# Fourteen gathered and eighteen dense columns per tile in the first layer of a two-layer graph network

## The reference, cut to what matters

```python
def layer0(x, W, b, src, dst):
    neigh_sum = segment_sum(x[src], dst, num_segments=N)
    deg = segment_sum(ones(E), dst, num_segments=N)
    mean = neigh_sum / maximum(deg, 1)[:, None]
    agg = where(deg[:, None] > 0, mean, x)
    return relu(concatenate([x, agg], -1) @ W.T + b)

x1 = layernorm(x + layer0(x, W, b, src, dst))
# layer 1: Q, K, V = x1 times a matrix chosen by node type; K of an edge also times a matrix
# chosen by edge type; softmax of Q[dst].K over the edges of each dst; sum of V[src] by it
out = layernorm(x1 + layer1(x1, src, dst, edge_type, node_type, ...))
```

## Time and profile before

| | |
|---|---|
| time, median of 3 runs | 3719.31 us (3719.02 to 3729.1) |
| time of the profiled execution | 3697.22 us |
| span of the profiled execution | 3695.4 us |
| mean granted TensorE clock | 0.839 of full speed |
| busy share | PE 69%, POOL 64%, DVE 41%, ACT 30% |
| first layer's steps, start to end | 99.4 to 1334.7 us |

### The profile page before, as it was taken

The page is one execution under the profiler, slowest core; times in us unless marked ns, Lnnn a source line. Parts: engine busy times, 40 slices in busy tenths (PEclk is TensorE's granted clock), DMA queues, the critical chain, the costliest instruction groups (busy, mean ns, idle before and its releaser), DMA issues.

```text
span 3695.4 us, 38864 instructions
## 1 busy us (share of the span) xinstructions
PE 2551.0 (69%) x13692; PEld 1754.7 (47%) x13692; DVE 1530.9 (41%) x4283; ACT 1124.1 (30%) x2072; POOL 2372.2 (64%) x2400
## 2 busy tenths in 40 slices
PE   1688888888888861666666666666676666666667
PEld 0355555555555541444444444444444444444445
DVE  8466666666666620222222222222222222222223
ACT  3333444444444420222222222222222222222222
POOL 6656667676666617566666666666666666666662
PEclk9799999999999985777777777777777777777778
DMA  4233344443444313233333333333333333333331
GB/s 135 64 98 115 107 130 120 119 120 107 120 120 120 112 68 107 72 96 96 97 97 96 97 97 96 97 97 96 97 97 97 97 97 96 96 97 97 97 97 43
DMA packets 195810, 369.81 MB, mean 100 GB/s; under 512 B 62177, under 2 KB 126509, under 8 KB 189347
## 3 DMA queue, kind: packets, MB, share of 16 engines
q0 software_dynamic: 112432, 281.92, 27.5%
q1 hardware_dynamic: 76679, 82.09, 6.7%
q10 hardware_dynamic: 6508, 3.33, 0.3%
HBM read 299.89 MB, written 67.30 MB: 99 GB/s over the span
## 4 chain that ended last, share of the span: by engine, by line
PE 38%; another core or an unknown queue 20%; issue 19%; ACT 14%; DVE 8%; ACTq 1%; DMA 0%; DVEq 0%; POOLq 0%; POOL 0%; SPq 0%
PE banks L715 8%; ACT work L1090 5%; PE banks L872 4%; PE banks L886 4%; PE banks L901 3%; PE banks L708 3%; ACT work L1098 3%; ACT picks L1007 2%; PE banks L738 2%; DVE sums L1269 2%; PE banks L771 1%; PE banks L908 1%; PE banks L866 1%; PE banks L776 1%
## 5 line engine op out<-in xcount | busy, mean ns | idle before, releaser
L655 POOL DMA_INDIRECT ring<-kv_table,src_n x1264 | 1207.9, 956 | 625.9 <-issue 368.8
L650 POOL DMA_INDIRECT ring<-x_part_rows,work x512 | 538.0, 1051 | 249.2 <-issue 138.4
L886 PE MATMUL banks<-identf,ring 128*128 128x128 f32 x1264 | 242.9, 319 | 646.5 <-ACT work L1098 458.2
L1007 ACT ACTIVATE picks<-banks 128x392 bf16<-128x392 f32 x800 | 396.6, 499 | 730.0 <-PE banks L708 646.7
L715 PE MATMUL banks<-sums,picks 128*128 128x385 bf16 x2450 | 617.6, 335 | 0.4 <-ACT picks L1007 0.4
L886 PEld LDWEIGHTS banks<-identf,ring 128*128 128x128 f32 x1264 | 169.4, 162 | 698.9 <-ACT work L1098 506.4
L1090 ACT ACTIVATE work<-banks,negmax 128x2048 f32<-128x2048 f32 x98 | 193.0, 1969 | 905.9 <-issue 668.4
L1098 ACT ACTIVATE work<-banks 128x512 f32<-128x512 f32 x392 | 213.0, 598 | 816.1 <-remote 689.1
L1467 DVE SCALAR_TENSOR_TENSOR sums<-sums,corr,banks 128x128 f32<-128x128 f32 x98 | 34.0, 347 | 936.5 <-remote 928.9
L1448 DVE TENSOR_REDUCE largest<-banks 128x1 f32<-128x2048 f32 x98 | 224.6, 2292 | 468.9 <-PE banks L872 252.3
L872 PE MATMUL banks<-work,queries 128*128 128x512 f32 x784 | 412.2, 674 | 4.1 <-issue 4.1
(11 more groups left out here) (279 smaller groups left out, 2785.7 us busy)
## 6 DMA issues: line engine op xcount, KB each, us to landing
kv_table<-ring SPq DMA_DIRECT2D x49, 1024.0 KB
ring<-kv_table,src_n POOLq DMA_INDIRECT x1264
ring<-x_part_rows,work POOLq DMA_INDIRECT x512
sums<-kv_table,src_n POOLq DMA_INDIRECT x304
x_part_rows<-sums SPq DMA_DIRECT2D x7, 675.5 KB, 4.5
src_n<-x_part_rows,work POOLq DMA_INDIRECT x256
sums<-x_rows SPq DMA_DIRECT2D x51, 64.0 KB, 1.9
x_rows<-ring SPq DMA_DIRECT2D x49, 64.0 KB
```

What stands on the lines that cost most here:

```text
L650: pool.indirect_dma_start(near[k % RUNS][:, j, :], None, part_dram, bass.IndirectOffsetOnAxis(ap=col_ids[:, first + j:first + j + 1], axis ...
L655: pool.indirect_dma_start(kv_ring[u][:, j, :], None, table, bass.IndirectOffsetOnAxis(ap=of, axis=0)).then_inc(l1_rows[2 * u + j // RUN], 16)
L886: tr = pe.transpose(bank[KEY_BANK[g]][:, j * P:(j + 1) * P], kv_ring[k.u][:, g * 4 + j, 0:D], identf[:, :])
L1007: act.activation(picked[:, par, :, c * NW:(c + 1) * NW], bank[c % 2][:, 0:KEYS].rearrange("p (h w) -> p h w", w=NW), ACT.Copy).then_inc(pi ...
```

## The change

- `NW` 8 to 7: a dense column covers 7 nodes. `GCOLS` 16 to 18: a dense group has 18 columns, 18 x 7 = 126 slots, so that `slot_sum` multiplies 126 of the 128 columns of weights, and a pick has 49 x 7 = 343 columns.
- Each tile has a fixed period of 32 columns: 14 gathered (two runs of `HALF` = 7), then 18 dense. All 49 steps are alike; the 50th is gone, and step 0 has runs too. The first layer gathers 686 columns in place of 768 and picks 882 in place of 800.
- `hot` works in batches of 3 with a ring of 9. The picks are spread evenly over the 49 slot sums (`PICK_AT` = 0, 3, 6, 9, 11, 14, ... 41, 44, 47). The runs stand at h=2 and 23, `node_sum` at 6, the parts of `late` at 9 to 29, those of `early` at 30, 36 and 42.
- DVE's order: after `join_parts` come `hot(i+1, 2)`, `belong`, `add_nodes`, `mean`, then the other batches. `hot(i+2, 1)` moves from behind `normalise_x1` to before it, so that `join_parts` is next after `normalise_x1`. ACT does `deviation` after take 16 of 18.
- After the last step the three tiles that are left are interleaved: the rest of tile 46 with the front of 47, the rest of 47 with the front of 48, then the rest of 48. The fronts have PSUM banks of their own.
- POOL: the keys of the edges (L636 to L640) come behind the first two runs of gathers. The far sweep comes behind the first eight gathers of block 0, and POOL waits for no scores in it. Layer 1 gathers 1563 columns, not 1568.

```diff
-NW = 8
-GCOLS = 16
-HOT_RING = 8
-BATCH = 4
+NW = 7
+GCOLS = 18
+HALF = 7
+PERIOD = 2 * HALF + GCOLS
+HOT_RING = 9
+BATCH = 3
...
-    ND = TILES + 1
+    ND = TILES
...
-            for k in range(2 * (ND - 2)):
+            for k in range(2 * ND):
+                if k == RUNS - 1:
+                    edge_keys()
+                    pool.wait_ge(keys_nat, 1)
...
-                first = (2 + 2 * (k // 2)) * GCOLS + k % 2 * RUN
-                for j in range(RUN):
+                first = gathered_cols(k // 2) + k % 2 * HALF
+                for j in range(HALF):
...
-                gate(pool, far_score_ps, it + 1)
-                pool.inc_swdge_sem([far_gathered], [32], mode="sub")
-
-            far_sweep(pool, lambda i: None, far, lambda i: None)
...
-                for j in range(COLS):
+                for j in range(min(COLS, NCOLS - b * COLS)):
+                    if b == 0 and j == RUN:
+                        far_sweep(pool, lambda i: None, far, lambda i: None)
...
-                mm = pe.matmul(bank[2 + i % 2][:, 0:3 * D + 1], picked[:, i % 2, h, :], x_parts[:, h, 0:3 * D + 1],
+                mm = pe.matmul(bank[2 + i % 2][0:SLOTS, 0:3 * D + 1], picked[:, i % 2, h, 0:SLOTS], x_parts[:, h, 0:3 * D + 1],
...
+            PICK_AT = [-(-c * TILES // GCOLS) for c in range(GCOLS)]
+            RUN_AT = (2, 23)
...
-                    if h == 3 and i > 0:
+                    if h == 6 and i > 0:
                         node_sum(i - 1)
...
-                        if h == 35:
+                        if h == 36:
                             transpose_mean(early)
-                        if h == 40:
+                        if h == 42:
                             first_product(early)
                     slot_sum(i, h)
+
+            def finish_and_begin(old, new):
+                transpose_typed(old)
+                transpose_mean(new)
+                project_keys(old, added(ND))
+                project_values(old)
+                first_product(new)
+                project_queries(old)
+                low_keys(old)
+                high_keys(old)
...
-                if early:
-                    deviation(early)
+                    if early and c == 16:
+                        deviation(early)
...
                 if i > 0:
                     join_parts(i - 1, (i - 1) % 2)
-                if runs_of(i + 1):
+                if i + 1 < ND:
+                    hot(i + 1, (i + 1) % 2, 2)
                     belong(i + 1, 0)
...
                     hot(i + 2, i % 2, 0)
                 if early:
                     relu(early)
-                    normalise_x1(early)
                 if i + 2 < ND:
                     hot(i + 2, i % 2, 1)
+                if early:
+                    normalise_x1(early)
```

## The result

The changed kernel took 3665.6 us (median of 4 runs, 3660.7 to 3669.2) beside 3720.5 for the kernel before: ratio 0.9847, 95% interval 0.9828 to 0.9866. It is faster, but by 55 us where 204.6 were forecast, and 3665.6 lies above the range. The profiled execution took 3660.7 us (span 3658.9).

The account below looks back on a forecast made before the run. PE bounds the step, with four waits in it. 181.2 + 16.8 + 2.6 + 12 - 11 + 0 + 3 = 204.6 us off the profiled 3697.2, plus 22.1 to the median: 3515 us, range 3480 to 3585.

Parts of the forecast that it names:

- The step's work and its four waits: First layer's step: PE's work 19.75 us; waits at L750, L755, L727 and L771, 4.07 us, shrink to 0.5.
- The wait ahead of slot sum 0: PE in each step: a new wait of 0.3 us, because take 17 comes behind `deviation`.
- The sizing of the steps: First layer's 46 full steps: 24.19 us each becomes 20.25, 3.94 less, 181.2 us in all.
- the rival with 0.04: Slower: in the first layer, gathers without pause bring gaps of 4.2 us; two per step give 3901 us; chance 0.04.
- 0.6 over 24.19: Full steps before average 24.8 us; the excess over 24.19 was taken as extra work in early steps that stays.
- 126 columns: Slot sums' weight load: a clock per column, hidden beside a 165 ns matmul, costs nothing; rival 3590 us, chance 0.03.
- POOL as the bound: Rival, first layer: gathers stretch beside more one-hots, POOL limits the step at 21.5 us, 3573 us; chance 0.16.
- The start: Start of first layer, to step 3's first run sum: gathering begins 10.2 us sooner, 12 us gained.
- The end of the layer: After the first layer's last step: 23.7 us becomes 34.6 with the interleaved tiles, 11 us lost.
- The second layer: Layer 1: earlier first gather taken as 0 gained; five gathers fewer at the end, 3 us gained.
- the prediction's signs of being wrong: Signs in the profile after; one was first values of layer 1 later than 125 us after its first gather.
- The waits stay: Rival: DVE's or ACT's order puts other waits in place; steps gain only 17 us, 3679 us; chance 0.03.

Follow-up runs that it names:

- free: Kind of session in which the kernel before took 3347 to 3353 us; the unmodified changed kernel had 0.9354 of it.
- held: Kind of session in which the kernel before took 3697 to 3726 us; the changed kernel had 0.9847, 0.9835 and 0.9603 of it.
- b126: Kernel before with slot sums of 126 weight columns, joins and node sums over 126 partitions; 3351.6 us, 0.9995 of the kernel before.
- after3: The changed kernel with nothing altered, measured again in the third session; 3555.2 us, 0.9603 of the kernel before.
- after4: The changed kernel with nothing altered, measured again in the fourth session; 3131.7 us, 0.9354 of the kernel before.
- nogather_b: Changed kernel where POOL gathers rows only for the first six runs of the first layer; 3453.2 us, 0.9346 of the kernel before.

## Why the prediction was right and wrong, step by step

**The step's work and its four waits: right.** Forecast 19.75 us of work and 0.5 of waits; measured 19.98 (free) and 19.87 (held, without gathers). In these steps nothing waits at L775, L780 or L796. At the node sum the forecast had the join at F + 3.4 and the release at F + 4.4. DVE's timeline of the free run, where relu starts at F + 0.1:

```profile
608.40 0.29 DVE L1361 SCALAR_TENSOR_TENSOR ring<-banks,ring 128x128 f32<-128x128 f32 x1 [0.50 <-PE banks L782]
...
610.38 0.15 DVE L1368 RECIPROCAL rstd<-rstd 128x1 f32<-128x1 f32 x1
611.66 0.28 DVE L1303 COPY sums<-banks 126x129 f32<-126x129 f32 x1
```

F, the start of PE's next slot sum, is 608.29: join at F + 3.37, node sum at 612.69 = F + 4.40. The wait ahead of slot sum 0 is there as well, 26.3 us in 50 places, 0.53 each for 0.3.

**The sizing of the steps: wrong, and this is the step that failed.** "So the step becomes 19.75 + 0.5 = 20.25 us, 3.94 less" took the whole of the four waits as time that their removal gives back. It does so in a free session. In the measured one the step is 23.95 us on average, and 64.6 us are gained for 200.6: 136 of the 168 us by which the sum was off. What stood in place of the four waits are PE's late signals.

The mechanism was written down, in the rival with 0.04: "the engines fall into the gaps that ACT shows at 113.12", decided by one such gap of 4.2 us in a step. Its price of 20.25 + 4.2 = 24.45 us for one gap is near 23.95, in part by luck: 92 late takes in 33 steps are nearly three a step, of 1.5 us on average. What the argument had against it was read wrongly. That PE has no such gap in the middle of the kernel before does not show that nothing is held there. Its record is in the earlier trace rows: 39.6 us of idle time ahead of takes that is put down to "issue". Between 200 and 1000 us the group reads so, kernel before held, then b126 (free), where nothing is put down to "issue":

```profile
L1007 ACT ACTIVATE picks<-banks 128x392 bf16<-128x392 f32 x515 | 256.1, 499 | 463.3 <-PE banks L708 430.0 <-issue 30.5 <-PE banks L715 2.1
```

```profile
L1007 ACT ACTIVATE picks<-banks 128x392 bf16<-128x392 f32 x515 | 256.4, 498 | 462.3 <-PE banks L708 462.1
```

And yet the median step of the kernel before is 24.2 and 24.3 us in its two held profiles, with 32 and 50 late takes, and 24.2 in the free one (b126) with none: in the middle of the layer a late signal costs nothing there, as PE stands still for 4.07 us a step anyway. So the four waits and the holds lay over each other, and in a held session taking the waits away gave only what was not covered.

A part of the held steps is the clock. At 620.2, after the wait of 1.88 us shown above, the granted clock falls to 0.5 (1.2 GHz) for 3.4 us. Of the 45 steps of the first held profile 19 have such a stretch; they take 25.8 us on average, the others 22.6. In the second 27 have one (25.1 and 23.1), in after3 8 (24.4 and 21.8), in the free changed kernel none. How much of such a step is the clock, and how much the long hold ahead of it, isn't separated.

The free session gained 29 us more in the steps than forecast (229.5). The "0.6 over 24.19" was taken as extra work that stays. In b126 11 of the 45 steps hold a stretch at half clock (26.3 us on average, the others 24.3), and without the waits the clock stays at 1.00: a part of the 0.6 was clock, and went.

**126 columns: the cost of nothing was right, its reason wrong.** The load does not take a clock per column, else 126 columns could not need 136 ns where 128 need 98. The Trainium skill (TensorE: Matmul & The Clock Gate, section "Weight-path perf modes — Fast Weight Load (FWL) and DoubleRow") has the fast load only for 128 weights that aren't FP32, and about twice as fast; the trace agrees in the direction, but 136 ns for 98 are a factor of 1.4. b126 shows that it costs nothing; 136 ns are still less than the 165 from one slot sum to the next.

**POOL as the bound: did not come.** More one-hots did not stretch the gathers: 1030 and 1031 ns on average in the free changed kernel, 1053 and 1069 in b126 (200 to 1000 us both). In a free step POOL waits 0.69 and 1.27 us for run sums (forecast: "about a microsecond"):

```profile
612.18 0.95 POOL L669 DMA_INDIRECT src_n<-x_part_rows,work  x1 [1.27 <-PE banks L758]
621.62 0.95 POOL L669 DMA_INDIRECT ring<-x_part_rows,work  x1 [0.69 <-PE banks L758]
```

**The start: wrong sign.** 12 us gained were forecast; 13.3 (held) and 17.4 (free) were lost. The first run sum of step 3 was put at 158 without waits from outside, 164 was taken, and it comes at 161.7 in the free session, but at 189.4 in the held one. The 176.06 of the kernel before, however, holds such waits itself; without them it is 144.3. First run sums of step 3, kernel before (b126) and changed kernel (after4), free:

```profile
144.29 1.00 PE L738 MATMUL banks<-ring 128*128 128x385 bf16 x5 [0.57 <-DMA ring<-x_part_rows,work]
```

```profile
161.71 0.98 PE L758 MATMUL banks<-ring 128*128 128x385 bf16 x5
```

A stretch with waits was compared with one reckoned without them. Steps 0 to 2 now have the runs of step 0 and take 22.7, 21.5 and 20.6 us for 13.7, 14.1 and 17.9.

**The end of the layer: right.** 9.8 to 12.7 us lost for 11, with a wait in it that the forecast didn't have: SP issues the load of the last tile's rows (at 1099.87) behind the stores of the one before (1099.03 and 1099.39), and PE waits for it.

```profile
1104.90 0.47 PE L770 MATMUL banks<-identf,ring 128*128 128x128 f32 x1 [6.57 <-DMA ring<-in_x_dram]
```

**The second layer: gained where nothing is held.** POOL starts 5.3 us behind the transposes of the keys for 17.0 before, 11.7 gained. With the five gathers fewer at the end it makes 17.9 us in all (1.1 and 16.7 in the table), for 3. That POOL's gathers carry the early start to the end fits the trace, where POOL waits for no buffer between 1500 and 3000 us; no run tested it. In the held session 2 us are lost. There one of the prediction's signs of being wrong came too: the first values stand 126.5 us after POOL's first gather, for 125 (121.6 before, 61.5 in the free session).

**The rival "The waits stay".** Its price of 3679 us is nearest to the result, but not for its reason: neither DVE's nor ACT's order puts a wait there.

**What stays open.** Which part of the gathers holds PE's signals (bytes, descriptors, or POOL's work for them), why only in some sessions, and why the changed kernel is at 0.984 in two held sessions and at 0.960 in a third. That the gathers do it is shown for the first layer (nogather_b). In the second, where the same part of the kernel before takes 2199 us held and 1957 free, PE's signals are held as well: between 1500 and 3000 us they come not more than 65 ns apart 162 to 195 times in every held profile, nogather_b among them, and never in a free one. POOL's gathers of the second layer, changed kernel held (after3), then free (after4), where nothing is put down to "remote":

```profile
L674 POOL DMA_INDIRECT ring<-kv_table,src_n x1259 | 1203.2, 956 | 684.5 <-issue 360.4 <-remote 232.4 <-SPq L531 68.0
```

```profile
L674 POOL DMA_INDIRECT ring<-kv_table,src_n x1259 | 1200.6, 954 | 450.1 <-issue 383.4
```

That the gathers are the cause there too is only argued, since no run took them away. No version that does all the work beat the changed kernel clear of noise in either kind of session.

## What to carry to other kernels

Before removing waits from an engine's schedule, look whether other engines are released late by it: idle time put down to "issue" or "remote" just behind that engine's work can be a second limit under the first, and the wait that you remove may be all that covers it. The times at which semaphores are raised tell it more directly. Take both sides of a difference from the same ground: a stretch full of such waits is not to be compared with one reckoned without. And where variants give more than their theory allows, compare the absolute time of the kernel before first; ratios from different sessions were not comparable here (0.9847 and 0.9354 for one kernel).

## What the hardware showed

- The kernel before takes 3347 to 3353 us in some sessions and 3697 to 3726 in others, steadily within each. Instructions are as long in both (a gather of the changed kernel's first layer 1.03 to 1.06 us, a take 516 ns); in the first layer the time is in late signals of PE and the clock that falls behind its waits.
- A matmul's recorded start did not tell when its signal comes: a pick recorded at 603.64 was taken 2.8 us later, and 1.0 us of complete rest of DVE, ACT and POOL stood beside a PE listed as busy. Held signals came in their order, 0.05 us apart.
- Weights of 126 bf16 columns load in 136 ns, of 128 in 98.
- In the second layer the mean granted clock was 0.78 of full speed in held sessions and 0.84 in free ones (1500 to 3000 us). In the first layer of the changed kernel (300 to 1000 us) it was 0.97, 0.96 and 0.99 held and 1.00 free; from 606 to 634 us of after3 it was 1.00 although takes were late.
